# Two attention blocks on one core: the input in two halves, other fillers, a later low-rank product, a wait per tap matrix

## What is computed

```python
x = x + _L0_conv_ref(_gn(x), ...)   # q, k, v = layer_norm(dwconv3x3(.)) of x @ w_qkv.T + b
x = x + _L1_conv_ref(_gn(x), ...)   # qkv plus a low-rank product on q and v

# in both, with 12 heads of 16 channels:
attn = jnp.einsum('bqc,bkc->bqk', q * scale, k) + rel_h[..., None] + rel_w[..., None, :]
o = softmax(attn) @ v
return o @ w_proj + b_proj          # block 0 adds q to o first

# in block 1
u = x @ FacTu_w
new_q = u @ q_facts_w @ FacTv_w
new_v = u @ v_facts_w @ FacTv_w
```

## Time and profile before

| | before |
|---|---|
| median of three executions | 109.63 us |
| lowest, highest | 109.55, 111.31 us |
| the profiled execution's own time | 108.68 us |
| its span, first to last instruction | 106.7 us |
| TensorE busy | 97.1 us, 91% |
| VectorE busy | 62.7 us, 59% |
| ScalarE busy | 51.3 us, 48% |
| GpSimd busy | 31.4 us, 29% |
| mean granted TensorE clock | 0.968 |
| moved by DMA | 3.73 MB |

### The profile page before, as it was taken

How to read it: one execution, slowest core, us unless ns; L and a number is a source line. 1 busy time by engine, 2 the same in 40 slices (tenths; PEclk the granted TensorE clock), 3 DMA queues, 4 the chain that set the end, 5 groups by cost and what they waited for, 6 DMA issues and landing times.

```text
span 106.7 us, 2097 instructions
## 1 busy us (share of the span) xinstructions
PE 97.1 (91%) x822; PEld 70.8 (66%) x825; DVE 62.7 (59%) x134; ACT 51.3 (48%) x115; POOL 31.4 (29%) x46
## 2 busy tenths in 40 slices
PE   5799999999959999999999999899989999999780
PEld 2155787578848986777856563797759879857440
DVE  3469995587999667834650135464796493560130
ACT  4011904663534981837815624254246668715820
POOL 8947600599999999000000000000000000000000
PEclk9995579999999999999999999999999999999999
DMA  2999980000000000000000000000000000000002
GB/s 59 308 307 292 237 79 0 3 0 6 0 0 0 9 0 0 0 0 6 0 0 0 0 6 0 0 0 0 0 0 6 0 0 6 0 0 0 0 0 74
DMA packets 2826, 3.73 MB, mean 35 GB/s; under 512 B 305, under 2 KB 2242, under 8 KB 2818
## 3 DMA queue, kind: packets, MB, share of 16 engines
q0 software_dynamic: 784, 0.79, 6.7%
q1 hardware_dynamic: 1282, 1.41, 4.8%
q10 hardware_dynamic: 752, 1.42, 4.5%
HBM read 3.42 MB, written 0.20 MB: 34 GB/s over the span
## 4 chain that ended last, share of the span: by engine, by line
PE 75%; DVE 10%; ACT 7%; DMA 3%; issue 2%
PE bank L917 9%; PE bank L760 8%; PE bank L853 6%; PE bank L850 6%; PE bank L749 6%; PE bank L892 5%; PE bank L905 5%; PE bank L866 5%; PE bank L893 4%; PE bank L831 3%; ACT pt L386 3%; DVE taps_m L622 3%; DMA x<-x_t 3%; PE bank L734 3%; PE bank L832 2%
## 5 line engine op out<-in xcount | busy, mean ns | idle before, releaser
L575 DVE TENSOR_REDUCE mx<-bank 128x2 fp32r<-128x512 f32 x24 | 15.0, 682 | 3.2 <-PE bank L866 3.2
L386 ACT ACTIVATE pt<-bank 128x512 f32<-128x512 f32 x24 | 13.0, 594 | 3.6 <-PE bank L893 3.4
L892 PE MATMUL bank<-qs,ks 128*128 128x256 f32 x48 | 13.3, 310 | 0.8 <-ACT pt L386 0.7
L570 DVE SCALAR_TENSOR_TENSOR qs<-qs,vec,bank 64x512 fp32r<-64x512 f32 x12 | 8.8, 737 | 6.9 <-ACT qs L376 6.8
L893 PE MATMUL bank<-mt,nhot_r 128*128 128x256 f32 x48 | 12.0, 280 | 0.0
L892 PEld LDWEIGHTS bank<-qs,ks 128*128 128x128 f32 x48 | 9.0, 187 | 2.8 <-ACT pt L386 1.8
L760 PE MATMUL bank<-pad,taps_m 128*128 128x256 f32 x36 | 10.5, 445 | 0.2 <-DVE taps_m L622 0.2
L734 PE MATMUL bank<-warm 128*128 128x512 bf16 x28 | 9.0, 443 | 1.5 <-POOL warm L279 1.3
L324 POOL TENSOR_SCALAR tap_p<-pad,vec 64x256 f32<-64x256 f32 (+1 forms) x11 | 10.3, 937 | 0.0
L749 PE MATMUL bank<-xn,w 96*128 96x256 f32 (+1 forms) x40 | 9.6, 428 | 0.6 <-DVE xn L549 0.6
L376 ACT ACTIVATE qs<-bank 64x512 fp32r<-64x512 f32 x12 | 7.1, 590 | 6.2 <-PE bank L853 6.2
(11 more groups left out here) (103 smaller groups left out, 166.7 us busy)
## 6 DMA issues: line engine op xcount, KB each, us to landing
ks<-hots POOLq DMA_DIRECT2D x1, 768.0 KB, 7.8
wp<-w_proj ACTq DMA_DIRECT2D x1, 576.0 KB, 8.1
w<-w_qkv SPq DMA_DIRECT2D x1, 432.0 KB, 8.8
w<-w_qkv SPq DMA_DIRECT2D x1, 288.0 KB, 4.8
cst<-consts ACTq DMA_DIRECT2D x1, 256.0 KB, 4.8
nhot<-neg_hot ACTq DMA_DIRECT2D x1, 256.0 KB, 5.7
x<-x_t SPq DMA_DIRECT2D x1, 192.0 KB, 3.3
wpq<-w_proj_q ACTq DMA_DIRECT2D x1, 192.0 KB, 8.9
```

Of the source, the lines that this page charges most:

```text
L386: act.activation(pt[:, h, :, :], key_banks[h % 2][:, :].rearrange("p (k n) -> p k n", k=QT), ACT.Exp).then_inc(exped[b], 1)
L575: dve.tensor_reduce(mx[:, h, :], ring_bank(h // 4, 4 + h % 4)[:, :].rearrange("p (q n) -> p q n", q=QT), AXX, ALU.max).then_inc(maxed[b], 1)
L892: pe.matmul(dst, ks[:, h, k * 128:(k + 1) * 128], qs[:, h, :], start=True, stop=False)
```

## The change

Four edits.

1. The input comes as two transfers: channels 0 to 95 at the head of SyncE's queue, channels 96 to 191 at the head of ScalarE's queue, ahead of `vec`. Each has its semaphore, and VectorE takes the statistics of a half once it is there.
2. `warm` is 128 columns wide instead of 512, and the filler reads it four times over, so that it still streams 512 columns. Eight fillers run before block 0's group sums instead of seven, and five behind them instead of four.
3. `lora_first` runs behind the convolution of A instead of ahead of the first projection.
4. `convolve` waits before tap k for k + 1 matrices, instead of once for nine. That holds for tile C too.

```diff
-        warm = sb("warm", [128, 512], mybir.dt.bfloat16)
+        warm = sb("warm", [128, 128], mybir.dt.bfloat16)
...
-            sp.dma_start(xs[0][0:HALF], x_t.rearrange("(t p) n -> p t n", p=HALF)).then_inc(d_x, 16)
+            sp.dma_start(xs[0][0:HALF, 0], x_t[0:HALF]).then_inc(d_x[0], 16)
...
             act.preload_act_table_set("natural_log_exp_and_others")
+            act.dma_start(xs[0][0:HALF, 1], x_t[HALF:]).then_inc(d_x[1], 16)
             act.dma_start(vec[:], vectors).then_inc(d_vec, 16)
...
             def group_norm_in(b):
-                if b == 0:
-                    dve.wait_ge(d_x, 16)
                 for t in range(2):
+                    if b == 0:
+                        dve.wait_ge(d_x[t], 16)
...
+            warm_row = warm[:, 0:1]
+            warm_again = bass.AP(warm_row.tensor, warm_row.offset, [list(warm_row.ap[0]), [0, 4], [1, 128]])
...
-                    pe.matmul(to[:, :], warm[:, 0:128], warm[:, :], start=True, stop=True)
+                    pe.matmul(to[:, :], warm[:], warm_again, start=True, stop=True)
...
                 if first == 0:
-                    pe.wait_ge(qtaps_set if v == 0 else vtaps_set, TAPS)
                     pe.wait_ge(padded, order0.index(t) + 1)
                 for k in range(first, last):
+                    pe.wait_ge(qtaps_set if v == 0 else vtaps_set, k + 1)
...
             pe.wait_ge(warm_set, 1)
-            warm_up(7)
+            warm_up(8)
             group_sums(0)
-            warm_up(4)
-            lora_first()
+            warm_up(5)
             pe.wait_ge(d_w0, 32)
             project(0, 0, A, w0)
             project(0, 1, B, w0)
             convolve(A, 0, 0, TAPS)
+            lora_first()
             project(0, 2, C, w0)
```

More of the change, by code:

```diff
@@ L169, in attention_blocks @@
         sum_sel = cst[:, SUM0:SUM0 + 128]
-        d_x, d_w0, d_cst, d_vec, d_w1 = map(sem, ("d_x", "d_w0", "d_cst", "d_vec", "d_w1"))
+        d_w0, d_cst, d_vec, d_w1 = map(sem, ("d_w0", "d_cst", "d_vec", "d_w1"))
+        d_x = [sem("d_x_0"), sem("d_x_1")]
         d_nhot, d_rel, d_lora, d_vb, d_wp, d_wpq = map(sem, ("d_nhot", "d_rel", "d_lora", "d_vb", "d_wp", "d_wpq"))
```

## The result

The change made the kernel slower: median 111.72 us (111.20 to 114.60, four executions) against 109.59 (109.41 to 111.31, four of the kernel before, run beside it), ratio 1.018, 95% interval 1.014 to 1.023. The forecast of 109.2 was wrong, and the time lies just beyond its range of 106.5 to 111.3. This ratio weighs only the undisturbed executions near each kernel's fastest, and where times scatter as these do it turns with the luck of those few: for twelve more executions of the same change it is 0.993 (0.987 to 1.000). So the comparisons further down take in every execution.

The account below looks back on a forecast made before the run. TensorE, 91% busy, bounds the kernel, with slow clock from 8.0 to 14.8 us. First variance 2.0 us earlier: 108.68 - 2.0 = 106.7; plus 2.5 for a clock loss behind the convolution: 109.2, range 106.5 to 111.3.

Parts of the forecast that it names:

- Part 1: Input in two halves at the kernel's head: group sums at 4.77, a gain of 0.45 us, ends -0.15 and 0.7.
- my worst case: Input transfers: vec also waits 0.75 us for the 96 KB ahead of it and lands at 5.35.
- Part 2: Fillers around the group sums: start at 0.97, eight and five of them hidden, cost zero, up to 0.05 us.
- the case that the forecast named as costing 0.4: Five fillers behind the group sums at the lower clock level: 2.15 us, to 7.3, costing 0.4.
- Part 3: Wait per tap matrix: first convolution no longer waits for all nine; no tap wait shows, extra waits zero, at most 0.6 us.
- Part 4: Low-rank product behind the convolution: ScalarE's copy and picks delay square A about 3.0 us, variance 3.4 after the convolution.
- The sum with the clock kept: Whole kernel at full clock: variance A at 15.8 against 17.82, 2.0 us earlier, 108.68 - 2.0 = 106.7.
- The failed step: Behind the first convolution: clock lost at some moment between 15 and 18, costing 2.5 us, giving 109.2; chance 0.42.
- the middle, 2.5: Price of the lost clock: between 1.7 us for a half-length slow stretch and 3.4 for a full one.
- my rivals: Clock kept throughout (106.7, chance 0.30); clock not kept at 8.0 (110.2 or 108.5, 0.16); long loss (112, 0.12).
- rival 3: Clock lost behind the convolution stays low through the first attention stage, some 10 us: price 112, chance 0.12.

Follow-up runs that it names:

- picks first: Full change with ScalarE's eight picks and square A ahead of the low-rank copy: median 108.08 us over 18 executions, 0.985 of the kernel before.
- vec first: Full change with vec ahead of x's second half on ScalarE's queue: median 112.89 us over six executions, 1.029 of the kernel before.
- f1_again: The full change measured again, nothing altered: median 111.61 us over twelve executions; the profiled execution took 110.19.
- e1_input: Only the input's two halves, on the kernel before: median 109.99 us over four executions, against 109.79 in its group.

## Why the prediction was wrong, point by point

**Part 1, the input: too high.** The halves landed 2.3 and 2.5 us after their issue, both by 3.3, so x was there earlier than I took (3.3 and 3.8), and the sums were ready at 4.17, not 4.65. But the page has, beside the earlier trace rows:

```profile
w<-w_qkv SPq DMA_DIRECT2D x1, 144.0 KB, 5.9
...
x<-x_t SPq DMA_DIRECT2D x1, 96.0 KB, 2.3
x<-x_t ACTq DMA_DIRECT2D x1, 96.0 KB, 2.5
...
vec<-vectors ACTq DMA_DIRECT2D x1, 80.5 KB, 4.2
```

`vec` took 4.2 instead of 3.4 and landed at 5.4, my worst case; the weights took 5.9 instead of 5.1 and landed at 7.54 instead of 6.75. Both terms I had left at their old durations. The first projection started at 7.65 instead of 6.9: a loss of 0.25 where I had a gain of 0.45. That size is one execution's: in the other profiled executions with this input, these fillers and the move, and with the clock up by then, it started between 7.13 and 7.42, against 7.40 before. So the part is worth between -0.25 and 0.3, and never its 0.45. The Trainium skill, DMA: Bandwidth & Descriptors, section Issuing engines are not separate DMA queues, has all transfers interleave on the same engines; the trace disagrees with what I drew from it for x, since the halves landed by 3.0 and 3.3 instead of 4.0, and agrees in that the transfers behind them took longer.

**Part 2, the fillers: right for the profiled execution, not for every one.** First at 0.98 (forecast 0.97), eight to 4.57, five in 1.24 us, all hidden; and the clock passed 8.0 at 1.00. Nine profiled executions have both the fillers and the halves at the head of both queues. In none did the clock fall between 7 and 14 us, but in three it had not yet risen: picks first until 9.76, and the two without the move until 13.28 and 15.58. In the first of these the five fillers took 2.29 us and the projection started at 8.14, which is the case that the forecast named as costing 0.4. Nor do the fillers alone hold the clock: without the halves it fell at 7.47, and with vec first at 7.99.

**Part 3, a wait per tap: right, but late by part 1.** The convolution started at 9.45 (forecast 8.6), while VectorE's ninth matrix ended at 10.89, and took 3.91 in the chain. No tap wait shows.

**Part 4, the move: right in its mechanism and size.** The convolution ended at 13.5, the square came at 16.29 and the variance at 16.70: 3.2 behind it, where I had 3.4. One row was read wrongly on the way: copy and picks did not lie inside ScalarE's wait of 3.87 us but ahead of it, from 11.06 to 13.12, beside the convolution; the result is the same.

**The sum with the clock kept: right to half a microsecond or so.** Forecast 106.7; the three executions of the full change with a full clock took 107.04 to 107.47. Part 1, wrong by 0.7 in the profiled execution and by 0.2 to 0.5 in the others, is of the size of that difference. In the profiled execution the variance came 1.12 sooner, not 2.0: 0.7 of the missing 0.9 is part 1, the rest small gaps ahead of the convolution and behind it.

**The failed step: the price, length and place of the lost clock.** I took "the middle, 2.5", between a half and a full stretch of 6.8 us, and only one moment for it, between 15 and 18. f1_again shows that moment (17.3) and a full stretch, which cost 3.1. But in 10 of 16 executions the clock was slow for 10.2 us or more, and the first profiled one has this at 46.2, in the attention stage, at 4.2 us instead of 2.5. 107.3 + 4.2 = 111.5, near the median of 111.69. That the one loss of f1_again fell in the forecast's place doesn't save the forecast: it came in one of two profiled executions. None of my rivals had a loss behind 22; rival 3 had the length, about 10 us, and its price of 112, but in the wrong place and at 0.12. I had read the full clock of the earlier trace rows from 14.8 to 106.7 as safety of the later stages. It was one execution: among 57 of the kernel before six had 0.954 or less. A smaller fault is that the sum stood on the profiled execution, 108.68, with the kernel's median over 61 executions at 109.75.

**What is open.** Why the move and the denser fillers together bring the long loss so much oftener, and why the clock rises late where the low-rank product comes early. For a link by way of the head's hole speaks that picks first has it in 4 of 18; against it, that TensorE's hole filled has it in 4 of 6. Three fillers at 43 us had it in 0 of 12 with the old order of ScalarE, and in 1 of 6 with picks first, so they may lower its frequency and do not exclude it. In unprofiled executions only the mean clock is known, not the place.

## What to carry to other kernels

When an operation is moved on one engine, move its reader on the other engine's list too: the copy that ScalarE could not start held up eight activations and the square behind it, and with one line moved a loss of 1.8% became a gain of 1.5%, most of it by way of the clock. Where the clock decides, look at the mean clock of many executions before and after: one profile shows one place where it fell, not how often or where else. Check the head by the duration of a pass that you know at either level, since the clock row can hide a slow one. A transfer brought to the head of a queue is paid by the one behind it; follow that one to its reader.

## What was unexpected of the hardware

The clock fell without an idle stretch ahead of it. TensorE in the change's profile, ahead of 46.2, first the stretch, then in order of time:

```profile
43.00:46.20 3.20, 3.20 (x35) 2.15 (x34) 1.61 (x4) 2.25 (x6) 0.00 (x0) 1.00 0.00 0
```
```profile
43.22 0.89 PE L1038 MATMUL bank<-lo_w,lo_t 16*96 16x192 f32 x4
...
44.25 0.65 PE L855 MATMUL bank<-qs,rel_w 64*64 64x64 f32 x8
44.74 0.69 PE L858 MATMUL bank<-qs,rel_w 64*32 64x32 f32 x16
45.36 0.64 PE L796 MATMUL bank<-conv_p,cst 64*64 64x256 f32 x2
```

It is busy for all of 3.20 us, with passes of 16 and 64 rows. These passes are not enough of a reason: the kernel before runs the same stretch of work 0.9 us later, and behind it the clock stayed at 1.00.

```profile
43.90:47.10 3.20, 3.20 (x35) 2.15 (x34) 1.61 (x4) 2.25 (x5) 0.00 (x0) 1.00 0.00 0
```

The Trainium skill, TensorE: Matmul & The Clock Gate, section Why this matters for your kernels, asks that long idle gaps be avoided. These falls are of another kind: none stands ahead of 46.2, and the longest ahead of 17.3 in f1_again was 1.37 us. The same kernel kept the clock in three executions of 16, as far as the record goes back, so what decides is not in the program alone. The late stretch, seen in four profiled executions (the change, the fillers alone, picks first with fillers, the hole filled), began at 45.7 to 47.2 and lasted 10.2 us each time; at 17.3 it was 6.8, as in the kernel before at 8.0, and four other falls, at 18.3, 26.9, 27.1 and 79.8, lasted 3.4.

Last, the clock row reads 1.00 until the first recorded change, though TensorE starts at 1.2 GHz: in e1_input that hid 16 us of slow clock, and in five other profiled executions 9.8 to 15.6 us. The kernel before lists 1.00 in 11 of 57 executions, and these took 109.45 to 110.93, no less than the others. By those profiles I take them for executions with a slow head; for these eleven that is argued, not shown.
